# A chunked delta-rule layer: 32x32 blocks done compactly, the inverse's last level in halves, and a new order of the slot

## What is computed

```python
q = l2(silu(conv(x @ Wq.T)));  k = l2(silu(conv(x @ Wk.T)));  v = silu(conv(x @ Wv.T))   # causal convolution, 4 taps
alpha = exp(-exp(A_log) * softplus(x @ Wa.T + dt_bias));  beta = 2 * sigmoid(x @ Wb.T)
for t in range(256):                       # per sequence and head, S is 64 x 128
    S = alpha_t * (S - beta_t * outer(k_t, k_t @ S)) + outer(k_t, v_t)
    o_t = q_t @ S
x = x + rms_norm(o).reshape(B, T, 2048) @ Wo.T
x = x + layernorm(x) @ sign(weight).T      # then a softmax attention and a top-2 mixture of experts
```

## Time and profile before

| what | us |
|---|---|
| median of 3 runs | 1286.54 (1285.4 to 1288.22) |
| profiled execution | 1296.63, span of its instructions 1294.8 |
| slots with q and k work (176.47 to 659.11, 19 slots) | 482.64, 25.40 each |
| slots without (715.37 to 882.86, 7 slots) | 167.49, 23.93 each |
| second layer and drain (from 945) | 350 |

### The profile page before, as it was taken

How to read it: one execution, slowest core, us unless ns; L and a number is a source line. 1 busy time by engine, 2 the same in 40 slices (tenths; PEclk the granted TensorE clock), 3 DMA queues, 4 the chain that set the end, 5 groups by cost and what they waited for, 6 DMA issues and landing times.

```text
span 1294.8 us, 32678 instructions
## 1 busy us (share of the span) xinstructions
PE 1147.9 (89%) x12540; PEld 842.7 (65%) x12540; DVE 925.0 (71%) x1785; ACT 814.3 (63%) x1462; POOL 644.5 (50%) x1192
## 2 busy tenths in 40 slices
PE   5779999999999999989999999998779887898991
PEld 1123677777767777767777777776555454798991
DVE  4757689988899989889976787776556658152232
ACT  5876787887888787898785666765243433333330
POOL 1015667767667776767774766674220102204314
PEclk9879699999999999999997999999889998899996
DMA  4012332221221122112212222240101011488982
GB/s 150 1 60 70 113 84 54 53 71 52 51 69 48 53 52 73 45 53 54 69 25 74 65 68 53 58 67 15 28 7 33 18 19 68 153 282 299 319 301 55
DMA packets 130106, 106.18 MB, mean 82 GB/s; under 512 B 59472, under 2 KB 116816, under 8 KB 129696
## 3 DMA queue, kind: packets, MB, share of 16 engines
q1 hardware_dynamic: 127904, 99.90, 27.1%
q0 software_dynamic: 2048, 4.20, 1.0%
HBM read 84.21 MB, written 15.73 MB: 77 GB/s over the span
## 4 chain that ended last, share of the span: by engine, by line
PE 60%; DVE 16%; issue 7%; ACT 7%; POOL 5%; DMA 2%; SPq 1%; POOLq 0%; DVEq 0%; ACTq 0%
PE pair L719 8%; PE bank L1015 6%; PE bank L757 4%; PE pair L683 3%; PE bank L1022 3%; PE bank L969 3%; PE bank L746 3%; PE pair L651 3%; PE bank L771 3%; PE bank L764 3%; DVE vc L1463 2%; PE bank L815 2%; PE bank L799 2%; PE bank L842 2%; DVE kc L1463 2%
## 5 line engine op out<-in xcount | busy, mean ns | idle before, releaser
L1880 POOL TENSOR_TENSOR SU<-SU 128x28 f32<-128x28 f32 (+6 forms) x448 | 197.4, 441 | 35.1
L1876 POOL TENSOR_TENSOR SU<-SU 128x28 f32<-128x28 f32 (+6 forms) x448 | 194.0, 433 | 35.3
L1463 DVE SCALAR_TENSOR_TENSOR vc<-vy,conv,vc 128x512 f32<-128x512 f32 x192 | 144.5, 753 | 6.0 <-ACT vc L1160 1.5
L1463 DVE SCALAR_TENSOR_TENSOR kc<-ky,conv,kc 128x512 f32<-128x512 f32 x162 | 127.0, 795 | 7.6 <-ACT kc L1134 5.1
L1776 DVE TENSOR_TENSOR vy<-bank,vc 128x512 f32<-128x512 f32 x46 | 31.8, 692 | 98.9 <-PE bank L1015 97.6
L719 PE MATMUL pair<-SM,KQ 64*128 64x128 f32 (+1 forms) x512 | 77.3, 380 | 23.0 <-DVE AM L1532 20.4
L1941 POOL TENSOR_TENSOR RR<-RR,nh 128x8 f32<-128x8 f32 x32 | 57.1, 1785 | 75.3 <-DVE RR L1583 72.3
L1855 POOL TENSOR_TENSOR st<-st,nh 128x4 f32<-128x4 f32 x16 | 16.6, 1040 | 146.8 <-DVE st L1439 110.1
L651 PE MATMUL pair<-xnT,WQ 128*128 128x512 f32 x128 | 76.3, 681 | 5.9 <-ACT qb L1134 5.1
L757 PEld LDWEIGHTS bank<-YP,PP 64*64 64x64 f32 x2048 | 66.6, 138 | 17.1 <-issue 12.7
L1532 DVE TENSOR_TENSOR AM<-pair,SM 128x512 f32<-128x512 f32 x76 | 48.9, 685 | 38.1 <-PE pair L719 34.9
(11 more groups left out here) (307 smaller groups left out, 3118.7 us busy)
## 6 DMA issues: line engine op xcount, KB each, us to landing
AM<-in_wex_dram SPq DMA_DIRECT2D x32, 768.0 KB, 5.1
SM<-dscr SPq DMA_DIRECT2D x58, 256.0 KB, 3.7
V<-in_wex_dram SPq DMA_DIRECT2D x14, 768.0 KB, 5.5
et<-dscr SPq DMA_DIRECT2D x38, 256.0 KB, 3.7
SM<-fscr SPq DMA_DIRECT2D x64, 128.0 KB, 2.9
scratch<-AM SPq DMA_DIRECT2D x128, 48.0 KB, 1.8
SU<-scratch SPq DMA_DIRECT2D x128, 32.0 KB
xs<-idle SPq DMA_DIRECT2D x2, 1472.0 KB, 9.7
```

Source lines behind the costliest of these rows:

```text
L1463: e.scalar_tensor_tensor(c, y[:, :, k:k + 256], conv[:, ct, k:k + 1], c, ALU.mult, ALU.add).then_inc(s_c, 1)
L1876: e.tensor_tensor(tmp[:, :, 0:k, 0:15 - k], sub[:, :, 0:k, k:k + 1].to_broadcast([128, 2, k, 15 - k]), sub[:, :, k:k + 1, k + 1:16].to_bro ...
L1880: e.tensor_tensor(sub[:, :, 0:k, k + 1:16], sub[:, :, 0:k, k + 1:16], tmp[:, :, 0:k, 0:15 - k], ALU.subtract).then_inc(s_su, 1)
```

## The change

**Blocks of 16.** SU is 512 wide in place of 1056: 16 partitions of each quarter hold one 16x16 block a step where 8 held two. `blocks` issues eight DMAs into SU in place of four, each of half the size. The 28 operations of `substitute` stay, over half the elements. The space of SU that the second layer used (GB) moves into tile V.

**From 16 to 32.** The blocks stand in compact tiles: Y0, X0, PP0 are 32 wide. `inv_a0` and `inv_b0` are 32 matmuls each with 32 rows, 32 weight columns and 16 moving columns, four to a j, one in each of the four diagonal 32x32 places of the array, where `inv_a` and `inv_b` with lv = 0 had 16 each with 64x64 weights and 32 moving columns. On DVE: `inv_turn` (transpose of 512), `inv_y0` (256), `inv_x0` (transpose of 256), `inv_p0` (128), `inv_s0` (128), `inv_w0` (spread to 64 columns, 512), `inv_x1` (transpose of 512).

**From 64 to 128.** `inv_c` does the j of head 0; `inv_cd` does one matmul of the other half of the first product and one of the first half of the second product in turn, which lie in opposite 64x64 places of the array; `inv_d` does the rest. ACT's `inv_n` is called for each half. Both products write to bank 5.

**Order.** All four loops are written anew. `vconv` is called tap by tap; k taps, v taps and steps of the inverse alternate. `inv_turn` stands ahead of the last two steps of am; `wout` and `inv_a1` come at the end of the slot, `inv_p1` at the start of the next; the exponentials of a unit are computed one slot earlier; `lengths` comes after the first `vproj`. `fill(4)` (dummy matmuls) of slots 31 to 35 is gone. `solve1` waits for the transpose in `rms1` and no longer for the step behind it. The semaphore s_fw is split in two, those of the convolutions in pairs.

```diff
-        SU = sb("SU", [128, 1056])
...
+        SU = sb("SU", [128, 512])
+        su2 = SU[:, :].rearrange("p (r x t) -> p r x t", r=16, x=2)
+        sub, tmp = su2[:, :, 0, :], su2[:, :, 1, :]
+        diag = SU[:, 0:496:33]
+        Y0 = sb("Y0", [128, NJ, 32])
+        X0 = sb("X0", [128, NJ, 32])
+        PP0 = sb("PP0", [128, NJ, 32])
...
                 if n:
-                    e.wait_ge(s_tt, n)
+                    e.wait_ge(s_i0, 3 * n - 2)
                 for a in range(4):
                     e.wait_ge(s_bo[a], 16 * n + 16)
-                    e.dma_start(SU[32 * a:32 * a + 8, 0:1024], scratch[a].rearrange("(m c) r t -> m c (r t)", c=3)[:, 0:2, :]).then_inc(s_bi, 16)
+                    rows = scratch[a].rearrange("(m c) r t -> m c (r t)", c=3)
+                    for h in range(2):
+                        e.dma_start(SU[32 * a + 8 * h:32 * a + 8 * h + 8, 0:496], rows[:, 0:2, 528 * h:528 * h + 496]).then_inc(s_bi, 16)
...
+            def inv_a0(n):
+                if n:
+                    e.wait_ge(s_ip, 2 * n)
+                e.wait_ge(s_ix, 2 * n + 1)
+                for j in range(NJ):
+                    for a in range(4):
+                        r = slice(32 * a, 32 * a + 32)
+                        ins = e.matmul(bank[4][r, 16 * j:16 * j + 16], N4(n)[r, j // 2, j % 2, r], X0[r, j, 0:16], start=True, stop=True)
+                ins.then_inc(s_ia, 1)
...
             def inv_c(n):
                 e.wait_ge(s_id, n + 1)
-                for j in range(NJ):
-                    ins = e.matmul(bank[4][64:128, j * 64:j * 64 + 64], block_of(n, j, 0, 64), XP[0:64, j, :],
-                                   start=True, stop=True)
+                for j in range(NJ // 2):
+                    ins = e.matmul(bank[5][64:128, j * 64:j * 64 + 64], block_of(n, j, 0, 64), XP[0:64, j, :], start=True, stop=True)
                 ins.then_inc(s_ic, 1)
 
+            def inv_cd(n):
+
+                e.wait_ge(s_in, 2 * n + 1)
+                for j in range(NJ // 2):
+                    c, d = NJ // 2 + j, j
+                    inc = e.matmul(bank[5][64:128, c * 64:c * 64 + 64], block_of(n, c, 0, 64), XP[0:64, c, :], start=True, stop=True)
+                    if j == NJ // 2 - 1:
+                        inc.then_inc(s_ic, 1)
+                    e.matmul(bank[5][0:64, d * 64:d * 64 + 64], XP[64:128, d, :], YP[64:128, d, :], start=True, stop=True)
+
...
+            def inv_w0(n):
+                e.wait_ge(s_iy, 2 * n + 1)
                 if n:
                     e.wait_ge(s_yfd, n)
                     e.wait_ge(s_yfc, 2 * n)
...
+                e.tensor_tensor(YP[:, :, :].rearrange("p j (y t) -> p j y t", y=2), Y0[:, :, :].unsqueeze(2).to_broadcast([128, NJ, 2, 32]),
+                                mask32.rearrange("p (y t) -> p y t", y=2).unsqueeze(1).to_broadcast([128, NJ, 2, 32]), ALU.mult).then_inc(s_i0, 1)
...
-                    e.tensor_tensor(tmp[:, :, 0:k, 0:15 - k], sub[:, :, 0:k, k:k + 1].to_broadcast([128, 2, k, 15 - k]),
-                                    sub[:, :, k:k + 1, k + 1:16].to_broadcast([128, 2, k, 15 - k]), ALU.mult).then_inc(s_su, 1)
+                    e.tensor_tensor(tmp[:, 0:k, 0:15 - k], sub[:, 0:k, k:k + 1].to_broadcast([128, k, 15 - k]),
+                                    sub[:, k:k + 1, k + 1:16].to_broadcast([128, k, 15 - k]), ALU.mult).then_inc(s_su, 1)
```

More of the change, by code:

```diff
@@ L572, in _ @@
             for n in range(NN):
-                if n and n + 1 < NN: spread(n + 1)
+                new = (n + 1) % NG == 0
+                if n and n + 1 < NN and not new: spread(n + 1)
                 if n + 1 < NN: exponents(n + 1)
                 blocks(n)
+                if n + 1 < NN and new:
+                    key_factors((n + 1) // NG)
+                    spread(n + 1)
                 if n % NG == NG - 2 and n + 2 < NN: factors((n + 2) // NG)
@@ L756, in inv_b @@
                         pq = slice(64 * q, 64 * q + 64)
[L757 removed]
+                        ins = e.matmul(half(bank[5][pq, j * 64:j * 64 + 64], 1, 1), PP[pq, j, :], half(YP[pq, j, :], 1, 1),
                                        start=True, stop=True)
@@ L1100, in _ @@
                 more(s, 7)
-                if has_w and has_g: wout(w, 1)
-                elif w < 0: fill(2)
-                if has_i: inv_b(i, 0)
+                if has_w: wout(w, 0)
+                if has_w: wout(w, 1)
+                elif w < 0: fill(4)
+                for it in PREP0.get(s, []): prep(*it)
                 if has_j: out(j, 0)
@@ L1106, in _ @@
                 more(s, 8)
-                if has_j: out(j, 1)
-                if has_g: vtr(2 * g)
+                if has_i: inv_a1(i)
+                if has_j and j >= NN - 3: out(j, 1)
                 more(s, 9)
@@ L1279, in _ @@
             e.activation(sgn[:, :], sgn[:, :], ACT.Sign).then_inc(s_sgn, 1)
-            e.wait_ge(s_zero, 3)
+            e.wait_ge(s_zero, 4)
+            for i in range(3):
+                exp(0, i)
             def item(kind, *a):
@@ L1374, in _ @@
-                more(s, 1)
-                if 0 < g < NN: vV(2 * g - 1)
-                if has_g: exp(g, 2)
-                if gap(s, "norm") is not None: norm(gap(s, "norm"))
-                more(s, 2)
-                more(s, 3)
-                if has_k: ksilu(2 * s)
+                has_n = 0 <= g and g + 1 < NN
+                if s % NG == 3 and 1 <= s // NG < NP: gates1(s // NG)
+                if has_l: lengths1(p)
+                if s % NG == 4 and 1 <= s // NG < NP: gates2(s // NG)
```

368 lines of the change are left out of this document (199 added, 169 removed).

## The result

The changed kernel takes 1300.9 us (median of 20 runs, 1291.45 to 1311.33) beside 1288.12 for the kernel before (20 runs). The ratio of the two is 1.0084, with a 95% interval of 1.0062 to 1.0107; the medians' own, 1.0099, lies inside it. The highest run counts as slow and is left out of the ratio. The kernel is slower by 13 us, where I forecast 43 us less, and lies outside the range. The profiled execution took 1303.96 us, its span is 1302.2 (before: 1296.63 and 1294.8).

The account below looks back on a forecast made before the run. PE was to bound slots with q and k on the mean (24.0 us), the loop plain slots (23.3) and those without (about 22): 28 plus 15, so 43 us off the median 1286.54 gives 1243.5 us; range 1218 to 1278.

Parts of the forecast that it names:

- The small products: PE's 32-block products: 64 records, four side by side, 0.65 us each instead of 1.05, saving 0.80 us a slot.
- the middle of the last level: PE's 16 records in pairs from opposite places of the array, 0.65 us, within 1.85 us for the level instead of 2.14.
- the 24.0 us that I forecast from PE: Mean slot with q and k: PE's 23.46 us of work plus 0.55 of waiting, against 25.40 before.
- the loop through copies, substitution, turn and am: Chain from one end of am to the next, a lower bound for the slot: 23.3 us (20.6 to 25.1).
- the loop is long: Rival: the chain takes 25.1 us, 23.3 without q and k, so only 11 us come off, 1275 us; 15%.
- Copies: From the end of am through writes and eight half-sized reads to POOL's start: 8.8 us, between 7.8 and 9.3.
- Substitution: POOL's memset and 28 operations over half the elements: 11.7 us, low end 10, high end 13, instead of 15.25.
- Without q and k: Slots without q and k work: loop about 22 us, PE 21.1, slot 22.2 against 23.93, 15 us over 9 slots.
- Filling the pipeline, draining it and the second layer: nothing: The parts outside the steady slots of the first layer were to bring no change in time.
- The clock: Rival: sparser PE work lowers the granted clock in each slot, costing 1.7 us a slot, 1290 us; 3%.

Follow-up runs that it names:

- e4: Changed kernel with half of POOL's substitution left out (rows 14 to 8 only, blocks not fully inverted); ratio 0.9779 to the kernel before.
- e2: Changed kernel with the key factors' five transfers issued between the block writes and the eight reads at the phase boundaries; ratio 1.0053 to the kernel before.
- e13: e12 with the key factors' five transfers issued ahead of the reads at the phase boundaries, as in e2; ratio 0.986 to the kernel before.
- e12: Changed kernel with four block reads of 24 partitions for eight, the twelve blocks as outermost dimension; ratio 0.9925 to the kernel before.
- e16: Changed kernel with the four dummy matmuls back ahead of `inv_b0` in slots 31 to 35; ratio 1.0116 to the kernel before.
- e5: The changed kernel measured again with nothing altered; ratio 1.0082 to the kernel before.

## Why the prediction was wrong

**What held.** The small products, and the start of `inv_cd`:

```profile
281.71 0.73 PE L764 MATMUL bank<-Y,PP 32*32 32x16 f32 x64
282.37 0.82 PE L835 MATMUL bank<-V,YF 128*128 128x128 f32 x5
...
302.12 0.27 PE L800 MATMUL bank<-XP,AM 64*64 64x64 f32 x1
302.13 0.27 PE L803 MATMUL bank<-YP,XP 64*64 64x64 f32 x1
```

From start to start 0.66 us for 64 records (forecast 0.65), and the middle of the last level 302.73 - 302.12 = 0.61 us for 16 (0.65). That is 10 ns a small record; the Trainium skill's page "TensorEngine Tiling (Array Packing)", section "Instruction Overhead", gives some 60 cycles a matmul. For records that go one after another that would be 25 ns each and 1.6 us a product, an estimate from that page, and the trace does not agree. Within each of the four places the 16 records follow each other at 41 ns, so such a cost in each place is not excluded. And where the round no longer bounds, slots with q and k do take the 24.0 us that I forecast from PE: 23.99 in e4, which leaves out half the substitution; without q and k it has 22.58 in the seven ordinary rounds, against 22.2. The place of the trouble was right too: the loop through copies, substitution, turn and am.

**The failed step: the loop's size.** The prediction had the loop, but added it up too short, at 8.8 + 11.7 + 2.8 = 23.3 us, so that PE's 24.0 us would bound. Over the 16 ordinary rounds from unit 4 to 22 (all but those of units 7 and 15) it was 9.5 + 12.65 + 2.8, with 0.1 between: 25.1 us. That is the rival "the loop is long" (25.1), to which I gave 15%.

- Copies, 8.8 against 9.5. The start of the reads I read from one slot, 1.96 us after the writes' issue. It was the shortest before: over units 4 to 21 the first read stood 2.0 to 3.4 us after am, 2.75 on the mean, and after it is 2.0 to 3.6 (in the late cases the fourth write's issue takes 1.9 us instead of 0.5). One slot, and the best one, was taken for all: that is 0.6 us. I also took a value between the full price of an issue (9.3) and a lower one for half-sized reads (7.8). The issues kept nearly the full price, 0.65 us each, 4.8 us from the first to the last where I had counted some 4.1; the last read then landed in 2.2 us, not 2.7.
- Substitution, 11.7 against 12.65. The chain is 9.7 us where no operation meets a tap of DVE (unit 31). Of all operations of the chain in this trace, 169 begin while a tap runs, and 155 of them take longer than others of their size, by 0.4 us on the mean and whatever the size. Of 100 that meet only a tap which begins after them two take longer, of 627 that meet none one does. Two neighbours of one size in the changed kernel:

```profile
241.48 0.78 POOL L1949 TENSOR_TENSOR SU<-SU 128x54 f32<-128x54 f32 x1
242.34 0.29 POOL L1953 TENSOR_TENSOR SU<-SU 128x54 f32<-128x54 f32 x1
```

  I had named that as the high end and taken the middle.
- Without q and k I forecast 22 for the loop and 22.2 for the slot; the seven ordinary rounds from unit 24 on took 23.45, so the 1.7 us a slot came to 0.5. There the loop was missed by less: copies 9.2, substitution 10.6 and 2.8 are 22.6. The other 0.9 us stands between substitution and turn, where in four of the seven rounds DVE comes late from its own steps.

**The step that was missing: the phase boundaries.** I counted the eight issues for the blocks and not for what is queued behind them on SP, the key factors, for which POOL waits. The rounds of units 7, 15 and 23 grew by 4.6, 4.2 and 1.4 us, together 10 us; e2 gives back 6 of them, which shows the queue; under the short reads e13 gives back 2.6 against e12. The question to ask was what each DMA behind the new issues is for, and who waits for it.

**"Filling the pipeline, draining it and the second layer: nothing".** Unit 4's am is 1.7 us late (unit 1's is 9.6 us late, since it now waits for the first turn; but unit 2's round, 31.42 us before, is 24.74, and most of it comes back). The rest is 3.3 us longer; its half-clock time is 104.6 us against 83.0. No run was aimed at it (the dummies of e16 stand ahead of it). It may count for more than these 3 us: e12 reaches unit 31 23 us before the profiled kernel before does, and is faster by 12 us as a whole; e2 reaches it 9.9 us before, and is slower by 8 us.

**The clock.** I gave it 3% as a cause by itself, from sparser products. From unit 4 to 31 there are 47.8 us at half clock where before had 20.5, and e4 shows that most of them go with the long round. At half the speed the 27 us more cost up to 14 us of PE work; how much of that lay on the path is open, since e16 got only 3 us for 14 us less. It may be much. Each execution has its mean granted clock on record; taken as time at half clock (an estimate, 2 x (1 - clock) x span) the changed kernel on e5's chip has 182 us on the mean of ten executions, the kernel before 132 us on the mean of thirteen. Among the executions of either kernel, one with 1 us more at half clock is longer by some 0.27 us. The 50 us between the two thus go with 13 us, and their medians differ by 10.5. Whether the low clock makes the time, or the same waits make both, is not shown.

The sum, change in the profiled span: 16 ordinary rounds from 25.5 to 25.15 us, -6; phase boundaries and the round of unit 22, +11; seven rounds without q and k, -3; start +2, rest +3: +7 us, where the forecast had -25 and -15 in the two stages. The medians differ by 13 us; the two profiled executions lie 8.5 and 3.1 us over theirs, and where the other 6 us are is not on record. Nor does any run have the compact blocks in the old order, so what the products give and what the order costs is not told apart. The price that I gave the long loop, 1275, was too low for the same reasons: it left out boundaries, start, rest and clock. In the 16 ordinary rounds it was right: 0.36 us less each, where it had 0.3.

## What to carry to other kernels

When an instruction that waits for a slow chain is put ahead of the one that feeds the chain's next turn, the whole chain becomes a lower bound of the period: add it up over many slots, not from the one that reads best, and compare it with the busiest engine before counting that engine's savings. More issues on a queue cost everyone behind them; list who. A transfer's landing depended on its outermost dimension here (5.0 us at 2, 2.5 at 12), so fewer, larger DMAs can be slower than many.
